# A routed feed-forward kernel on one core: GpSimd's scatters spread between its additions, and waits for landings in the last two pairs

## What is computed

```python
def reference(x, ids, ...):
    z = relu(x @ Wd[ids] + bd[ids])
    y = x + z @ Wu[ids] + bu[ids]
    h = layernorm(y) * g[ids] + b[ids]
    probs = softmax(h @ gate_w + gate_b)
    values, experts = top_k(probs, 2)          # values normalised to sum 1
    moe = sum over the two experts e of value_e * (gelu(h @ ew1[e] + eb1[e]) @ ew2[e] + eb2[e])
    return x + h + (gelu(h @ sh_w1 + sh_b1) @ sh_w2 + sh_b2) + moe
```

## Time and profile before

| | us |
|---|---|
| median of 3 runs | 654.41 |
| lowest and highest | 653.47, 654.74 |
| the profiled execution | 652.95 |
| its span, first to last instruction | 650.9 |
| TensorE busy | 599.8 |
| VectorE busy | 503.1 |
| GpSimd busy | 413.1 |

### The profile page before, as it was taken

The page is one execution under the profiler, slowest core; times in us unless marked ns, Lnnn a source line. Parts: engine busy times, 40 slices in busy tenths (PEclk is TensorE's granted clock), DMA queues, the critical chain, the costliest instruction groups (busy, mean ns, idle before and its releaser), DMA issues.

```text
span 650.9 us, 16857 instructions
## 1 busy us (share of the span) xinstructions
PE 599.8 (92%) x5073; PEld 484.5 (74%) x5073; DVE 503.1 (77%) x1198; ACT 389.3 (60%) x662; POOL 413.1 (63%) x320
## 2 busy tenths in 40 slices
PE   4356999999989899999999999999999999999994
PEld 2223666766646668888888888888888888889883
DVE  3859889979975793898989898988896665656883
ACT  1638666667767774667675858576754444434641
POOL 2435687788887601285959585858688575756743
PEclk9768999999989999999999999999999999999998
DMA  7964467666144756367657585666686342424410
GB/s 265 304 145 133 128 190 151 215 195 154 57 126 121 247 160 191 84 125 134 147 105 155 126 142 130 137 133 129 90 71 73 52 73 44 67 41 59 69 26 3
DMA packets 116740, 81.31 MB, mean 125 GB/s; under 512 B 71090, under 2 KB 106162, under 8 KB 116658
## 3 DMA queue, kind: packets, MB, share of 16 engines
q1 hardware_dynamic: 101346, 61.16, 38.4%
q0 software_dynamic: 13296, 16.92, 15.3%
q10 hardware_dynamic: 2016, 2.16, 1.1%
HBM read 43.21 MB, written 24.42 MB: 104 GB/s over the span
## 4 chain that ended last, share of the span: by engine, by line
PE 71%; DVE 9%; issue 7%; POOL 4%; ACT 3%; DMA 3%; SPq 2%; POOLq 0%; ACTq 0%; DVEq 0%
PE H L1219 29%; PE Y L1235 29%; PE Y L1170 6%; PE H L1158 6%; SPq L287 2%; POOL xs_rows L430 2%; DVE wreg L768 1%; DMA xT<-wreg 1%; POOL wreg L413 1%; DVE wreg L737 1%; DMA wreg<-in_wpack 1%; DVE wreg L734 1%; DVE wreg L828 1%; ACT hf L554 1%; ACT wreg L501 1%
## 5 line engine op out<-in xcount | busy, mean ns | idle before, releaser
L608 ACT ACTIVATE hf<-H,prme 128x256 f32<-128x256 f32 (+1 forms) x312 | 151.0, 541 | 112.1 <-issue 97.4
L1219 PE MATMUL H<-xT,wreg 128*128 128x256 f16 (+1 forms) x1872 | 200.4, 263 | 0.2
L1235 PE MATMUL Y<-wreg,hh 128*128 x1136 | 188.6, 273 | 3.6 <-issue 2.4
L1219 PEld LDWEIGHTS H<-xT,wreg 128*128 x1872 | 171.9, 98 | 21.1 <-issue 0.7
L1235 PE MATMUL Y<-wreg,hl 128*128 x568 | 154.8, 273 | 0.0
L1235 PEld LDWEIGHTS Y<-wreg,hh 128*128 128x128 f16 x1136 | 111.0, 98 | 20.6 <-issue 6.1
L1031 DVE SCALAR_TENSOR_TENSOR hl<-hf,prme,hh 128x512 f16<-128x512 f32 (+1 forms) x156 | 115.1, 738 | 5.6
L1029 DVE TENSOR_SCALAR hh<-hf,prme 128x512 f16<-128x512 f32 (+1 forms) x156 | 84.6, 542 | 40.4 <-ACT hf L608 38.3
L457 POOL TENSOR_SCALAR b2w<-b2t,wsel 128x256 f32<-128x256 f32 x71 | 99.1, 1606 | 23.6 <-DMA b2t<-in_b 18.1
L1158 PE MATMUL H<-xT,wreg 128*128 128x512 f16 x384 | 93.8, 396 | 11.8 <-DMA xT<-wreg 11.7
L468 POOL DMA_INDIRECT out_y<-hh,xgm x36 | 64.7, 1799 | 58.0 <-DVE hh L1057 38.9
(11 more groups left out here) (189 smaller groups left out, 672.9 us busy)
## 6 DMA issues: line engine op xcount, KB each, us to landing
stage<-in_w SPq DMA_DIRECT2D x16, 1024.0 KB
b2t<-in_b SPq DMA_DIRECT2D x39, 128.0 KB
wreg<-in_wpack SPq DMA_DIRECT2D x16, 256.5 KB
wreg<-in_xt SPq DMA_DIRECT2D x16, 256.0 KB
wreg<-in_x SPq DMA_DIRECT2D x16, 256.0 KB, 5.6
wreg<-in_vecs SPq DMA_DIRECT2D x16, 256.0 KB, 4.0
out_y<-wreg SPq DMA_DIRECT2D x16, 256.0 KB, 2.2
xs_rows<-wreg SPq DMA_DIRECT2D x9, 260.0 KB
```

What stands on the lines that cost most here:

```text
L608: act.activation(hf[:, c, half * w:(half + 1) * w], H[c][:, half * w:(half + 1) * w], ACT.Gelu_apprx_tanh, bias=pr[:, ch:ch + 1], scale=pr ...
L1219: m = pe.matmul(H[c][:, half * w:(half + 1) * w], we[:, bass.ds(e + h * 2048 + k * 1024 + col, P)], xp[:, a + k, 0:w], start=i == 0, stop= ...
L1235: m = pe.matmul(Y[n % 2][:, j * D:(j + 1) * D], hx[:, n % 2, c * w + j * P:c * w + (j + 1) * P], we[:, bass.ds(e + 4096 + h * 2048 + c * D ...
```

## The change

Only GpSimd's program is changed. `scatter` now issues one DMA (p, i, q). For pairs 0 to 5 the 48 scatters are put singly between the additions of steps 4 to 25. For pairs 6 and 7 the places in the loop stay, but the first scatter of each block waits: block 0 of pair 6 for seven scatters of pair 5, block 0 of pair 7 for all of pair 6, and every other block for the block ahead of it.

```diff
-            def scatter(p, i):
-                pool.wait_ge(v_pos, p + 1)
-                pool.wait_ge(v_meta, p + 1)
-                pool.wait_ge(v_xl, p + 1)
-                pool.wait_ge(q_tok, p + 1)
-                for q in range(2):
-                    pool.indirect_dma_start(xs_d, bass.IndirectOffsetOnAxis(pos[:, p % 3, i, q:q + 1], 0), xr[:, p % 3, i, :].bitcast(I32), None).then_inc(d_row[p % 3], 16)
+            def scatter(p, i, q):
+                if (i, q) == (0, 0):
+                    pool.wait_ge(v_pos, p + 1)
+                    pool.wait_ge(v_meta, p + 1)
+                    pool.wait_ge(v_xl, p + 1)
+                    pool.wait_ge(q_tok, p + 1)
+                if p >= NP - 2 and q == 0 and i:
+                    pool.wait_ge(d_row[p % 3], 16 * (8 * (p // 3) + 2 * i))
+                elif p == NP - 2 and q == 0:
+                    pool.wait_ge(d_row[(p - 1) % 3], 16 * (8 * ((p - 1) // 3) + 7))
+                elif p == NP - 1 and q == 0:
+                    pool.wait_ge(d_row[(p - 1) % 3], 16 * 8 * ((p - 1) // 3 + 1))
+                pool.indirect_dma_start(xs_d, bass.IndirectOffsetOnAxis(pos[:, p % 3, i, q:q + 1], 0), xr[:, p % 3, i, :].bitcast(I32), None).then_inc(d_row[p % 3], 16)
...
             for s in range(FIRST, NS):
+                even(s, 14, 3, 0)
+                odd(s, 15, 3, 1)
                 for p in at(s, 3):
                     root(p)
+                odd(s, 14, 2, 1)
+                even(s, 13, 1, 1)
                 for p in at(s, 5):
                     rows(2 * p)
+                odd(s, 12, 0, 0)
+                even(s, 12, 0, 1)
+                for p in at(s, 5):
                     rows(2 * p + 1)
...
-                for p in range(NP):
+                for p in range(NP - 2, NP):
                     for i in range(4):
-                        if s == base(p) + (11 + i if p < NP - 2 else 10 + i // 2):
-                            scatter(p, i)
+                        if s == base(p) + 10 + i // 2:
+                            scatter(p, i, 0)
+                            scatter(p, i, 1)
```

## The result

| | before | after |
|---|---|---|
| median, us | 654.40 | 670.83 |
| lowest and highest | 653.47, 654.74 | 669.90, 672.53 |
| the profiled execution, and its span | 652.95, 650.9 | 672.53, 670.6 |
| TensorE, VectorE, GpSimd busy | 599.8, 503.1, 413.1 | 605.0, 512.9, 420.4 |

The ratio is 1.0256, with a 95% interval from 1.0231 to 1.0282 (four runs each). The direction was forecast, the size was not: 670.8 lies above the range of 656.0 to 665.5.

What follows compares the result with a forecast made beforehand. TensorE was taken as the bound, with SyncE's first expert transpose having 0.7 us of slack. Spreading at nothing and waits at +7.0 us took the profiled 652.95 to 660.0, median 661.4 us; range 656.0 to 665.5.

Steps and rivals of the forecast that it cites:

- What bounds the kernel: TensorE is the busy engine; three places left: stall at 182 (4.9 us), passage to the experts (slack 0.7 us), 270 to 280.
- the clock behind the wait: After TensorE's 6.3 us wait ahead of the first expert GEMM1, a lowered clock costs 1.7 us more.
- the two stretches named for "no gap": TensorE in steps 22 to 31: 34.97 busy of 35 us from 190, and 15.44 of 15.5 from 228.
- Part one: Spreading the scatters of pairs 0 to 5 between GpSimd's additions: second L413 addition up to 1.3 us later, costed at nothing.
- The cover of 3.3 us: At pair 6, ScalarE's L509 ended 3.3 us before VectorE's L768 began, so a 1.3 us delay would not show.
- a matter of phase: Number of VectorE encounters with GpSimd additions, unchanged in count; each worth 1.6 us up or down, only in the range.
- Part two: Pairs 6 and 7, each block's scatters waiting for the landing ahead: 4.86 us a block, SyncE's expert transpose 7.0 us later.
- the block behind the stage loads: Pair 6's block 6.2, its second scatter amid SyncE's stage loads: 7.9 us, landing at about 220.5.
- The pads' term of 0.9 us: SyncE's pads run beside blocks 7.0 to 7.2 and delay scatters there; 0.9 us added in all.
- The start of pair 6, 203.8: Its first scatter, at 203.07 before, waits for seven of pair 5's eight scatters and so begins at 203.8.
- "The landings are slower": Rival: pads and stage loads delay pair 7's blocks, pair 6 starts later; +4 more, 664 to 668 us; chance 0.14.
- "The stall at 182 closes": Rival: spreading frees VectorE ahead of pair 6's transposes, gaining 4.9 us; 656.5 us with waits as priced, chance 0.08.

Runs made afterwards that it cites:

- e1: The changed kernel without its waits for landings: scatters of pairs 0 to 5 spread between additions, pairs 6 and 7 as before; 1.0081 to the kernel before.
- e10: The kernel before with landing waits in pairs 6 and 7, and VectorE's lower halves of stages 2 and 3 cut to 64 of 2048 columns; 1.0175.
- e2: The kernel before with the landing waits in pairs 6 and 7 and nothing else, pair 6 waiting for all eight scatters of pair 5; 1.0236.
- e12: The kernel before with VectorE's low parts of pair 6's rows made ahead of the statistics of block 15 in step 20; 0.9968.
- e5: The kernel before with landing waits in pair 6 alone and VectorE's lower halves of stages 2 and 3 cut to 64 of 2048 columns; 1.0035.
- e4: The kernel before with the landing waits in pair 6 alone; 1.0147, median 663.27 us.
- e9: The kernel before with landing waits in pair 6 alone, VectorE's lower halves of units 2 and 3 made by a one-input operation; 1.0058.
- e11: The changed kernel whole, with VectorE's lower halves of stages 2 and 3 cut to 64 of 2048 columns; 1.0199 to the kernel before.
- e7: The changed kernel without landing waits, scatters still spread, but the two additions of L413 (rows) put together again; 1.0052 to the kernel before.
- e3: The kernel before with the landing waits in pair 7 alone; 1.0114, median 661.89 us.

## Why the prediction was wrong, by its own steps

- **What bounds the kernel: right.** The passage had hardly any slack, 2.0 us came back behind it (1.3 forecast), and the clock behind the wait cost 2.2 us where 1.7 were taken. One reading is off: the two stretches named for "no gap" leave out 225 to 228, where TensorE stands 1.9 us (from 225.38) ahead of its L1092. It stands 1.9 us there after the change too, so the difference does not come from it.
- **Part one, costed at nothing: wrong, 5.3 us.** The cover of 3.3 us was read on ScalarE's L509. The loss came on another path, VectorE's queue. The prediction had the mechanism in hand (the row of 1.81 us on VectorE beside an addition) and called the number of meetings a matter of phase, up or down. But with a scatter between two additions VectorE starts in the gap and then meets the second addition, as the rows at 159.38 and 170.52 show; its busy time rose by 8.7 us in `e1`. That the range took 1.6 us either way was too little for additions in 25 steps.
- **Part two, the block of 4.86 us: nearly right undisturbed** (4.51 in `e10`, 3.98 and 4.31 for the first two in after), and the block behind the stage loads too (7.9 forecast, 7.82 in after, 8.75 in `e10`). The waits by themselves cost 8.7 us against 7.0. The pads' term of 0.9 us for three blocks was too small: two blocks in pair 7 took 6.00 and 7.14 us in `e10`, 3.4 us more than 4.86 twice. How much of that is pads and how much VectorE wasn't taken apart.
- **The start of pair 6, 203.8: wrong in after** (213.95), since part one and the start of this execution had already shifted TensorE by about 7 us and pair 5's scatters are spread behind it. In `e2`, without part one, it was 207.48, with a wait for all eight scatters of pair 5; in `e1`, without the waits, 210.97, where it was 203.07 before; 1.5 of these 7.9 us lie ahead of the first scatter. So some 6 of the 10 us are part one's.
- **The missing term: 4.5 us by the last block of after (9.31 for 4.86), 6.4 by the ratios.** The prediction asked who waits for the scatters and what stands behind them on GpSimd, but not what they would run beside at their new times. Past 236 VectorE works on the stages without a gap, and GpSimd's scatters cannot get through. In the trace of before they begin at 236.31 and 239.76, 9 us after the last scatter has begun, so nothing there showed the conflict; the waits moved the scatters onto them.
- **The rivals.** "The landings are slower" gave the nearest time (up to 668) for the wrong reason: the landings are about as forecast, the issuing is what became slow. "The stall at 182 closes" did not come: in after TensorE waits 3.1 us for L843 at 166 to 169 and then 1.4 us (3.2 before) for pair 6's transposes, 4.5 in all where 0.8 and 3.2 made 4.0. That the stall's price would turn into gain in full was also wrong, by `e12`.

In sum: 7.0 forecast, plus 1.7 for the waits, 6.7 for the meeting and 5.3 for spreading, less some 4 of overlap, is 16.8. That it closes is no check, since the meeting and the overlap are differences of the same ratios. The terms come from ratios with intervals of about half a per cent each, so single ones may be off by 2 to 4 us.

Two things stay open beside those named. In `e5` the eight pads took 15.06 us on SyncE where they take 8.7 to 9.4 in before, after, `e2` to `e4` and `e9` to `e11`, and left a wait of 2.5 us for TensorE. And the start of the kernel up to the first scatter took 2.1 us more in the profiled execution of after than in that of before, and 0.2 to 1.8 us more in those of `e1` to `e4`, `e7` to `e9` and `e12`; what moves the landing of the first loads was not looked into.

## What to carry to other kernels

When a wait delays work, price it in two steps: when it runs then, and beside what. An indirect DMA of GpSimd is cheap only where VectorE leaves it room; one that slid under three long back-to-back operations on SBUF took 4.5 to 6.8 us instead of 1. And before breaking up a run of GpSimd operations to let something in between, count who else uses the gaps: each of the pieces may now meet VectorE alone.

## What the runs showed of the hardware that was not expected

- A scatter that met VectorE's long back-to-back operations on the stages was not slowed in proportion but held off until the next one that reads PSUM began, or, for the one after it in after, until the last one ended. In five traces it ended 0.91 to 0.93 us after the start of the operation on Y: 250.27 for 249.36 (after), 242.48 for 241.57 (`e2`), 245.29 for 244.36 (`e3`), 242.66 for 241.74 (`e4`), 241.71 for 240.79 (`e9`). Alone it takes 0.97 us. The prediction had weighed what GpSimd's additions do to VectorE, and did not turn it round for the scatters.
- The seams between VectorE's own operations (each starts before the one ahead has ended by its row) gave a waiting scatter no chance there. That is no general rule. In `e1` a scatter ended at 202.10, 0.93 us after the start of L797, which has two inputs in SBUF, reads no PSUM and began at such a seam; `e5` has the same at 193.98. What decides at a seam stays open. VectorE, and the scatter:

```profile
199.97 1.28 DVE L995 SCALAR_TENSOR_TENSOR hl<-hf,prm,hh 128x1024 f16<-128x1024 f32 x1 [0.72 <-ACT hh L591]
201.17 1.28 DVE L797 SCALAR_TENSOR_TENSOR wreg<-wreg,sm 128x1024 f16<-128x1024 f32 x1
```

```profile
200.39 1.71 POOL L430 DMA_INDIRECT xs_rows<-wreg  x1 [0.30 <-issue]
```

- A block of two scatters that waits for the landing of the one ahead had a period of 4.5 to 4.7 us undisturbed (pair 6's first) in `e2`, `e4`, `e5`, `e9` and `e10` (3.98 and 4.31 in after), and of 7.4 to 9.1 us in these and after when 2 MB of loads were issued ahead of it.
